# Another order of work for all engines in the transformer stacks: the four groups of small products stand apart

## The chip, the cores and the metric

The kernel runs on one core of a Trainium2 chip. The metric is the device time of one launch in microseconds (us), the median of several runs. TensorE does the matrix products (PE in the profile; PEld is its weight load), VectorE is DVE, ScalarE is ACT, GpSimd is POOL, and SyncE (SP) issues the DMAs. Each engine runs its own instructions in the order in which they are written, and waits on semaphores for the others.

## The reference, cut to what matters

The input x is 4 sequences of 512 tokens with 128 features, float32. Four blocks are added to x one after the other: a retention attention, a stack of six layers, a recurrent mixer, and the same stack again. Only the two stacks are touched here. A layer of the stack is

```
q, k, v = split(shift(x) @ Wqkv)          # 16 heads of 64
q, k = rotary(l2norm(q) * qs), rotary(l2norm(k) * ks)
# windows of 32 queries against the 64 keys of the window before and their own
attn = softmax(mask(8 * q @ k.T)); x = (attn @ v) @ Wo + x
a, gate = split(layernorm(shift(x)) @ W1 + b1)
x = a * gelu(gate) @ W2 + b2 + x
```

## The kernel before, in words

`ffn_stack` (line 347) computes a stack. It is built twice, for the two stacks. Its unit of work is a tile of 128 tokens: 96 tiles per stack (6 layers, 4 sequences, 4 tiles each), 192 in all. Four tiles make a group, for which the feed-forward part is done at 512 columns.

On TensorE a tile needs: six projections `project` (line 577; chunks k0, q0, k1, q1, v0, v1; each 128x128 times 128x512), four times `turn` (585; four 128x128 transposes each), the scores `scores` in two parts (600; 64 small products of 64x64 by 64x32 in all, 8 window-and-row places for 8 head pairs; the trace counts two matmuls and two weight loads for each), two times `turn_probs` (611; four transposes), the values `weigh` in two parts (626; 32 small products each, two matmuls and two loads for each), and `project_out` (640; eight 128x128 products, again two matmuls each). A group adds `center` (647), `variance` (654), six `up` (661) and `down` (670, three products): 11 products of 128x512.

Around them: VectorE does `rotate` (1018, 1020), `sum_squares` (1029), `norms` (1041 to 1052), `mask_max` (1063; it frees the score banks `bank_s`), `sum_probs` (1073), `invert` (1081), `mid` (1091), `mid_norm`, `hidden` and `finish`. ScalarE does `square` (855), `guess`, `keep` (881), `values_out` (889), `exponent` (898), `probs_out` (905), `heads_out` (913) and the group's activations. GpSimd does `stage` (1192), `rope` (1200), `unit` (1210), `off_max` (1218) and `scale_probs` (1226). SyncE spreads the values to their windows by DMA (`spread_values`) once both `values_out` of a tile and `weigh` part 1 of the tile two before it are done, and prefetches the weights of the next layer.

The order is written out by hand, per engine, in a function `slot(N, T, G, at, of)`: one slot per tile, T is N modulo 4. `at(lag)` names the tile that is `lag` slots behind, `of(lag)` the group. So the engines work at several tiles at once: on TensorE before, a slot does the first projections of tile N and the output projection of tile N-6. `slots` (469) writes out 16 slots, then a loop of two rounds of 32 slots, then 28 slots.

The results of projections and transposes go to four PSUM banks `work[0..3]`. TensorE uses them in turn, and ahead of each use waits until the reader of the bank's last content is done; `BANK` tells the readers which bank to take. The scores go to `bank_s[0..1]`, which both parts write and both `mask_max` read; the values go to `bank_o`, which each part of `weigh` fills and `heads_out` empties.

Before, TensorE's slot holds `weigh` part 0 by itself near its start, and `weigh` part 1, `scores` part 0 and `scores` part 1 directly one behind the other near its end.

Of the kernel before, what the change touches and what calls it, by code (L numbers as in the profile page):

```python
# [346 lines left out]
def ffn_stack(nc, shared, w):  # L347

    xo, ident, rot, mask = shared["x"], shared["ident"], shared["rot"], shared["mask"]
    with ExitStack() as ctx:  # L350
# [3 lines left out]
        def ps(name):  # L354
# [58 lines left out]
            "wa1": 3,  # L413
            "t_q0": (1, 3, 2, 1),
            "t_k1": (2, 1, 3, 2),
            "t_q1": (3, 2, 0, 3),
            "p_q0": (0, 3, 0, 3),
            "p_k0": (1, 0, 1, 0),
            "p_v1": (1, 3, 2, 3),
            "wo": (0, 3, 1, 0),  # L420
            "p_v0": (3, 1, 0, 1),
            "wg2": 0,
            "p_q1": (2, 1, 1, 0),
            "pt0": (0, 3, 3, 2),
            "p_k1": (0, 3, 3, 2),
            "t_k0": (2, 0, 3, 2),
            "pt1": (3, 0, 2, 1),
            "wa2": 2,
            "wa0": 3,
            "ct": 2,  # L430
            "va": 3,
            "w2": 3,
            "wg1": 0,
            "wg0": 2,
        }
        FIRST_IN, LAST_IN, LAST_UNIT, FIRST_PV, LAST_PV = "q0", "v0", "q1", 0, 1
# [131 lines left out]
        def _(pe):  # L568
# [104 lines left out]
            def slot(N, T, G, at, of):  # L673
                row = of(0).row
                if T == 0:
                    wait(pe, "pt_set0", N - 5)
                    up(of(3), "lin", 1, work[(0 + row) % 4])
                    wait(pe, "ot_set1", N - 6)
                    weigh(*at(5), 0)
                    wait(pe, "squared_k1", N - 1)  # L680
                    turn(*at(2), "q0", work[(1 + row) % 4])
                    wait(pe, "kept_k0", N - 2)
                    turn(*at(2), "k1", work[(2 + row) % 4])
                    wait(pe, "pt_set1", N - 5)
                    turn(*at(2), "q1", work[(3 + row) % 4])
                    wait_group(pe, "hid1", G - 3)
                    project(*at(0), "q0", work[(0 + row) % 4])
                    wait(pe, "kept_q0", N - 2)
                    project(*at(0), "k0", work[(1 + row) % 4])
                    wait(pe, "kept_k1", N - 2)  # L690
                    project(*at(3), "v1", work[(2 + row) % 4])
                    wait(pe, "kept_q1", N - 2)
                    project_out(*at(6), work[(3 + row) % 4])
                    wait(pe, "squared_q0", N - 0)
                    project(*at(3), "v0", work[(0 + row) % 4])
                    wait(pe, "squared_k0", N - 0)
                    up(of(3), "gate", 2, work[(1 + row) % 4])
                    wait(pe, "v_out1", N - 3)
                    project(*at(0), "q1", work[(2 + row) % 4])
                    wait(pe, "mid_set", N - 6)  # L700
                    turn_probs(*at(4), 0, work[(3 + row) % 4])
                    wait(pe, "v_out0", N - 3)
                    project(*at(0), "k1", work[(0 + row) % 4])
                    wait(pe, "ot_set0", N - 5)
                    weigh(*at(5), 1)
                    wait(pe, "masked1", N - 3)
                    scores(*at(2), 0)
                    scores(*at(2), 1)
                    wait_group(pe, "gelu2", G - 3)
                    turn(*at(1), "k0", work[(1 + row) % 4])  # L710
                    wait(pe, "squared_q1", N - 0)
                    turn_probs(*at(4), 1, work[(2 + row) % 4])
                elif T == 1:
                    wait(pe, "pt_set0", N - 5)
                    up(of(3), "lin", 2, work[(3 + row) % 4])
                    wait(pe, "ot_set1", N - 6)
                    weigh(*at(5), 0)
                    wait(pe, "squared_k1", N - 1)
                    turn(*at(2), "q0", work[(0 + row) % 4])
                    wait(pe, "kept_k0", N - 2)  # L720
                    turn(*at(2), "k1", work[(1 + row) % 4])
                    wait(pe, "pt_set1", N - 5)
                    turn(*at(2), "q1", work[(2 + row) % 4])
                    wait_group(pe, "hid2", G - 3)
                    project(*at(0), "q0", work[(3 + row) % 4])
                    wait(pe, "kept_q0", N - 2)
                    project(*at(0), "k0", work[(0 + row) % 4])
                    wait(pe, "kept_k1", N - 2)
                    project(*at(3), "v1", work[(1 + row) % 4])
                    wait(pe, "kept_q1", N - 2)  # L730
                    project_out(*at(6), work[(2 + row) % 4])
                    wait(pe, "squared_q0", N - 0)
                    project(*at(3), "v0", work[(3 + row) % 4])
                    wait(pe, "squared_k0", N - 0)
                    up(of(3), "lin", 0, work[(0 + row) % 4])
                    wait(pe, "v_out1", N - 3)
                    project(*at(0), "q1", work[(1 + row) % 4])
                    wait(pe, "mid_set", N - 6)
                    turn_probs(*at(4), 0, work[(2 + row) % 4])
                    wait(pe, "v_out0", N - 3)  # L740
                    project(*at(0), "k1", work[(3 + row) % 4])
                    wait_group(pe, "hid0", G - 3)
                    center(of(2), work[(0 + row) % 4])
                    wait(pe, "ot_set0", N - 5)
                    weigh(*at(5), 1)
                    wait(pe, "masked1", N - 3)
                    scores(*at(2), 0)
                    scores(*at(2), 1)
                    wait(pe, "squared_q1", N - 0)
                    variance(of(2), work[(1 + row) % 4])  # L750
                    wait(pe, "pt_set0", N - 4)
                    turn(*at(1), "k0", work[(2 + row) % 4])
                    wait(pe, "squared_k1", N - 0)
                    turn_probs(*at(4), 1, work[(3 + row) % 4])
                elif T == 2:
                    wait_group(pe, "center_set", G - 2)
                    down(of(3), work[(0 + row) % 4])
                    wait(pe, "ot_set1", N - 6)
                    weigh(*at(5), 0)
                    wait_group(pe, "std_read", G - 2)  # L760
                    turn(*at(2), "q0", work[(1 + row) % 4])
                    wait(pe, "kept_k0", N - 2)
                    turn(*at(2), "k1", work[(2 + row) % 4])
                    wait(pe, "pt_set1", N - 5)
                    turn(*at(2), "q1", work[(3 + row) % 4])
                    wait_x(pe, G - 3)
                    project(*at(0), "q0", work[(0 + row) % 4])
                    wait(pe, "kept_q0", N - 2)
                    project(*at(0), "k0", work[(1 + row) % 4])
                    wait(pe, "kept_k1", N - 2)  # L770
                    project(*at(3), "v1", work[(2 + row) % 4])
                    wait(pe, "kept_q1", N - 2)
                    project_out(*at(6), work[(3 + row) % 4])
                    wait(pe, "squared_q0", N - 0)
                    project(*at(3), "v0", work[(0 + row) % 4])
                    wait(pe, "squared_k0", N - 0)
                    project(*at(0), "q1", work[(1 + row) % 4])
                    wait(pe, "v_out1", N - 3)
                    turn_probs(*at(4), 0, work[(2 + row) % 4])
                    wait(pe, "mid_set", N - 6)  # L780
                    project(*at(0), "k1", work[(3 + row) % 4])
                    wait(pe, "ot_set0", N - 5)
                    weigh(*at(5), 1)
                    wait(pe, "masked1", N - 3)
                    scores(*at(2), 0)
                    scores(*at(2), 1)
                    wait(pe, "v_out0", N - 3)
                    turn(*at(1), "k0", work[(0 + row) % 4])
                    wait(pe, "squared_q1", N - 0)
                    turn_probs(*at(4), 1, work[(1 + row) % 4])  # L790
                elif T == 3:
                    wait(pe, "pt_set0", N - 5)
                    up(of(2), "gate", 1, work[(2 + row) % 4])
                    wait(pe, "ot_set1", N - 6)
                    weigh(*at(5), 0)
                    wait(pe, "squared_k1", N - 1)
                    turn(*at(2), "q0", work[(3 + row) % 4])
                    wait(pe, "kept_k0", N - 2)
                    up(of(2), "gate", 0, work[(0 + row) % 4])
# [47 lines left out]
        def _(act):  # L847
# [110 lines left out]
            def slot(N, T, G, at, of):  # L958
                keep(*at(2), "k0")
                probs_out(*at(5), 1)  # L960
                if T == 3:
                    gelu(of(2), 1)
# [1379 lines left out]
```

## Time and profile before

| | us |
|---|---|
| median of 3 runs | 3958.96 (3957.44 to 3965.38) |
| the profiled execution's own time | 3964.79 |
| its span in the trace | 3963.0 |
| PE busy | 3592.3 (91%) |
| DVE busy | 3253.2 (82%) |
| POOL busy | 2634.9 (66%) |
| ACT busy | 2372.4 (60%) |

The busy shares are averages over both stacks, the mixer between them (about 1800 to 2260 us) and the retention block ahead of them. In the page's 40 slices PE stands at nine tenths or more in nearly all slices of the stacks, DVE at eight, POOL at seven or eight.

### The profile page before, as it was taken

Reading aid. Unit: us, or ns where it says so; the run is one execution under the profiler, and the core shown is the slowest. Engines: PE = TensorE matmul, PEld = TensorE weight load, DVE = VectorE, ACT = ScalarE, POOL = GpSimd, SP = SyncE. Lnnn points to the kernel's source line nnn. Section 1 sums busy time; section 2 is a strip of 40 time slices with the busy share of each in tenths; the row PEclk is TensorE's granted clock in tenths of the full one; section 3 lists DMA queues with packets and bytes.
Section 4 is the critical chain, followed back from the end, with each engine's and each line's share of the span. In section 5 each row is a group of like instructions: output and inputs, shape, how many; then the busy total and the mean of one; then the engine's idle time right before and its main releaser. Section 6 shows DMA issues by size and latency. Waiting matters only on the chain. (4 is left out here: it accounts for less than half of the span.)

```text
span 3963.0 us, 156885 instructions
## 1 busy us (share of the span) xinstructions
PE 3592.3 (91%) x61680; PEld 2388.6 (60%) x61680; DVE 3253.2 (82%) x11525; ACT 2372.4 (60%) x4337; POOL 2634.9 (66%) x2556
## 2 busy tenths in 40 slices
PE   6799999999999999987699589999999999999997
PEld 4466666666666666652465356666666666666664
DVE  6888888888888888854899688888887888888884
ACT  2466667666666666663422156666666667666664
POOL 1787878877788778743000188787877788877872
PEclk9899999999999999997799689999999999999999
DMA  1232322322322322220000023233232232322222
GB/s 52 59 82 68 81 73 73 80 71 68 79 73 72 78 72 67 67 56 15 1 1 6 28 64 80 62 84 77 71 80 67 73 82 73 78 71 70 66 65 55
DMA packets 170283, 250.91 MB, mean 63 GB/s; under 512 B 36544, under 2 KB 67264, under 8 KB 169408
## 3 DMA queue, kind: packets, MB, share of 16 engines
q1 hardware_dynamic: 169536, 240.72, 24.4%
q8 instruction: 497, 8.14, 0.9%
q14 instruction: 250, 2.05, 0.2%
HBM read 38.21 MB, written 1.05 MB: 10 GB/s over the span
## 5 line engine op out<-in xcount | busy, mean ns | idle before, releaser
L1200 POOL TENSOR_TENSOR stack_roped<-stack_rot_c,stack_rot_s 128x512 f32<-128x512 f32 x768 | 966.3, 1273 | 420.9 <-DVE stack_rot_s L1020 420.9
L577 PE MATMUL stack_work<-stack_w_qkv,stack_xs 128*128 128x512 f32 x2304 | 1122.1, 603 | 36.3 <-ACT stack_sq L855 21.0
L1210 POOL TENSOR_TENSOR stack_roped<-stack_roped,stack_rnorm 128x512 f32<-128x512 f32 x768 | 784.6, 1043 | 175.9 <-DVE stack_rnorm L1052 175.9
L1018 DVE TENSOR_TENSOR stack_rot_c<-stack_work,rot_tables 128x512 f32<-128x512 f32 x768 | 518.3, 675 | 259.7 <-PE stack_work L577 256.5
L855 ACT ACTIVATE stack_sq<-stack_work 128x512 f32<-128x512 f32 x768 | 451.2, 598 | 367.7 <-DVE stack_rot_s L1020 367.6
L577 PEld LDWEIGHTS stack_work<-stack_w_qkv,stack_xs 128*128 128x128 f32 x2304 | 396.6, 193 | 335.1 <-issue 323.7
L626 PEld LDWEIGHTS stack_bank_o<-stack_p_t,stack_v_w 64*64 64x64 f32 x24576 | 405.4, 136 | 314.9 <-issue 308.8
L1063 DVE CUSTOM_DVE_ANT_0 stack_s_m<-stack_bank_s,band 128x64 f32<-128x64 f32 x3072 | 469.6, 218 | 137.4 <-PE stack_bank_s L600 126.0
L1029 DVE TENSOR_REDUCE stack_ssq<-stack_sq 128x8 f32<-128x512 f32 x768 | 519.8, 677 | 6.9 <-issue 6.6
L1020 DVE TENSOR_TENSOR stack_rot_s<-stack_work,rot_tables 128x512 f32<-128x512 f32 x768 | 522.0, 680 | 0.0
L1218 POOL TENSOR_TENSOR stack_s_m<-stack_s_m,stack_smax 128x512 f32<-128x512 f32 x384 | 421.2, 1097 | 114.9 <-DVE stack_smax L1063 113.5
L626 PE MATMUL stack_bank_o<-stack_p_t,stack_v_w 64*64 64x32 f32 x24576 | 452.1, 222 | 15.3 <-issue 14.3
L585 PE MATMUL stack_work<-ident,stack_roped 128*128 128x128 f32 x3072 | 436.0, 283 | 18.9 <-issue 13.9
L881 ACT COPY stack_q_t<-stack_work 128x512 f32<-128x512 f32 x384 | 228.4, 595 | 351.1 <-PE stack_work L585 350.8
L640 PEld LDWEIGHTS stack_work<-stack_o_t,stack_w_o 128*128 128x128 f32 x3072 | 372.7, 192 | 96.0 <-issue 94.9
L600 PE MATMUL stack_bank_s<-stack_k_t,stack_q_t 64*32 64x64 f32 x24576 | 322.2, 225 | 112.0 <-issue 111.5
L1226 POOL TENSOR_TENSOR stack_s_m<-stack_s_m,stack_inv 128x512 f32<-128x512 f32 x384 | 400.8, 1044 | 9.4 <-DVE stack_inv L1081 9.4
L585 PEld LDWEIGHTS stack_work<-ident,stack_roped 128*128 128x128 f32 x3072 | 343.7, 143 | 94.5 <-issue 66.4
L640 PE MATMUL stack_work<-stack_o_t,stack_w_o 128*128 128x128 f32 x3072 | 374.4, 275 | 3.6 <-issue 1.9
L600 PEld LDWEIGHTS stack_bank_s<-stack_k_t,stack_q_t 64*32 64x32 f32 x24576 | 275.5, 105 | 142.5 <-issue 133.3
L661 PE MATMUL stack_work<-stack_x_c,stack_w 128*128 128x512 f32 (+1 forms) x576 | 312.2, 625 | 23.6 <-issue 15.4
L881 ACT COPY stack_k_t<-stack_work 128x512 f32<-128x512 f32 x384 | 224.6, 585 | 147.4 <-PE stack_work L585 141.9
(247 smaller groups left out, 5193.0 us busy)
## 6 DMA issues: line engine op xcount, KB each, us to landing
stack_v_w<-stack_v_nat SPq DMA_DIRECT2D x1152, 128.0 KB
stack_v_w<-stack_v_nat SPq DMA_DIRECT2D x768, 64.0 KB
stack_w_qkv<-table_ffn_qkv SPq DMA_DIRECT2D x192, 96.0 KB, 2.1
stack_w_o<-table_ffn_wo SPq DMA_DIRECT2D x12, 512.0 KB, 4.4
stack_w<-table_ffn_w SPq DMA_DIRECT2D x12, 384.0 KB, 3.2
stack_w<-table_ffn_w SPq DMA_DIRECT2D x12, 192.0 KB, 2.9
x_outer<-L_attn_a_X SPq DMA_DIRECT2D x4, 256.0 KB, 7.5
ret_xpos<-table_xpos SPq DMA_DIRECT2D x1, 1024.0 KB, 6.8
```

What stands on the lines that cost most here:

```text
L577: pe.matmul(bank[:, :], xs[:, T, :], w_qkv[:, g.half, col:col + 512], start=True, stop=True).then_inc(done["proj_" + c], 1)
L585: last = pe.transpose(bank[:, P * n:P * (n + 1)], roped[:, CHUNKS.index(c), T % 2, P * n:P * (n + 1)], ident[:, :])
L600: last = pe.matmul(bank_s[j][WINDOW * n:WINDOW * (n + 1), 64 * hp:64 * hp + 64], q_t[rows, T % 2, hp, WINDOW * n:WINDOW * (n + 1)], k_t[ro ...
L626: last = pe.matmul(bank_o[HD * odd:HD * (odd + 1), gp, at:at + WINDOW], v_w[64 * gp:64 * gp + 64, T % 2, n, 2 * m + j, :], p_t[64 * gp:64 ...
L640: last = pe.matmul(bank[:, 0:P], w_o[:, g.half, n, :], o_t[:, T % 2, n, :], start=n == 0, stop=n == PAIRS - 1)
L881: act.copy(out, src).then_inc(done["kept_" + c], 1)
L1018: dve.tensor_tensor(rot_c[:, i % 2, :].rearrange("p (h d) -> p h d", h=8), src.rearrange("p (h d) -> p h d", h=8), cosine, ALU.mult)
L1020: dve.tensor_tensor(rot_s[:, i % 2, :].rearrange("p (h f d) -> p h f d", h=8, f=2), src.rearrange("p (h f d) -> p h f d", h=8, f=2)[:, :, ...
L1029: dve.tensor_reduce(ssq[:, T % 2, i, :], sq[:, i % 2, :].rearrange("p (h d) -> p h d", h=8), AX.X, ALU.add).then_inc(done["summed_" + c], 1)
L1063: last = dve.tensor_tensor_reduce(s_m[:, T % 2, j, hp, :], bank_s[j][:, 64 * hp:64 * hp + 64], mask[:, first:first + 2 * WINDOW], 1.0, LOW ...
L1200: pool.tensor_tensor(roped[:, i, T % 2, :], rot_c[:, i % 2, :], rot_s[:, i % 2, :], ALU.add).then_inc(done["roped_" + c], 1)
L1210: pool.tensor_tensor(r, r, rnorm[:, T % 2, i, :].unsqueeze(2).broadcast_to([P, 8, HD]), ALU.mult).then_inc(done["united_" + c], 1)
```

## The change

Only the order and the lags change; no operation is added or dropped. On TensorE a slot now reads, without its waits (T = 1; the feed-forward products of the other T stand at like places):

```
project q1 (tile N-3), up, project v1 (N-5),
weigh part 1 (N-7),
turn q0, turn k0 (N-4), turn_probs 1 (N-6), turn q1 (N-4), project k0, project q0 (N-2),
scores part 0 (N-4),
turn_probs 0 (N-6), project_out (N-7),
weigh part 0 (N-6),
turn k1 (N-4), project k1 (N-2), project v0 (N-4),
scores part 1 (N-4), up
```

The core of the diff:

```diff
-        FIRST_IN, LAST_IN, LAST_UNIT, FIRST_PV, LAST_PV = "q0", "v0", "q1", 0, 1
+        FIRST_IN, LAST_IN, LAST_UNIT, FIRST_PV, LAST_PV = "k0", "v1", "k1", 0, 1
...
-                    wait(pe, "ot_set0", N - 5)
-                    weigh(*at(5), 1)
-                    wait(pe, "masked1", N - 3)
-                    scores(*at(2), 0)
-                    scores(*at(2), 1)
...
+                    wait(pe, "ot_set0", N - 7)
+                    weigh(*at(7), 1)
...
+                    wait(pe, "masked1", N - 5)
+                    scores(*at(4), 0)
+                    wait(pe, "pt_set1", N - 6)
+                    turn_probs(*at(6), 0, work[(0 + row) % 4])
+                    wait(pe, "kept_q1", N - 4)
+                    project_out(*at(7), work[(1 + row) % 4])
+                    wait(pe, "ot_set1", N - 7)
+                    weigh(*at(6), 0)
...
+                    project(*at(4), "v0", work[(0 + row) % 4])
+                    scores(*at(4), 1)
```

The table `BANK`, the four `slot` functions of TensorE (T = 0 to 3) and those of ScalarE, VectorE and GpSimd are rewritten to match. The one of VectorE, new:

```
mid_norm, finish (T == 2); sum_squares k1, q1 (N-2); norms 0 (N-2); hidden 1 (T == 1);
rotate k0, q0 (N-1); norms 1; mid (N-6); norms 2; sum_squares k0 (N-1); norms 3;
sum_probs 1 (N-4); rotate k1 (N-1); sum_probs 0; invert 1; sum_squares q0 (N-1);
hidden 2 (T == 0) or hidden 0 (T == 3); rotate q1 (N-1); invert 0; mask_max 0, 1 (N-3)
```

The one of ScalarE: center_out and inv_std (T == 3), gelu 1 (T == 1), square q1, values_out 1, keep q0 and k0, heads_out 1, gain_bias (T == 3), probs_out 1, keep q1, table load (T < 2), guess, probs_out 0, exponent 0, square k0 and q0, exponent 1, heads_out 0, keep k1, center_square (T == 2), square k1, gelu 2 (T == 0), values_out 0, gelu 0 (T == 3). The one of GpSimd: stage, rope k0 and q0, unit q0 and k0, scale_probs 1, unit q1, scale_probs 0, rope k1 and q1, off_max 0, unit k1, off_max 1. A slot of VectorE or GpSimd runs beside TensorE's slot of the next number. The down product of a group moves from T == 2 to T == 3.

## Rows read from the trace of the kernel before

**Rows 1.** Busy time of each engine in a steady stretch (x instructions), clock, DMA.
```profile
300.00:1500.00 1200.00, 1140.41 (x21952) 773.70 (x21951) 1016.86 (x3888) 800.72 (x1474) 938.73 (x910) 0.99 0.30 74
```

**Rows 2.** TensorE's groups in the same stretch: count | busy, mean ns | idle before.
```profile
L626 PE MATMUL stack_bank_o<-stack_p_t,stack_v_w 64*64 64x32 f32 x8960 | 164.3, 221 | 4.5 <-issue 4.2
L585 PE MATMUL stack_work<-ident,stack_roped 128*128 128x128 f32 x1120 | 159.3, 283 | 7.1 <-issue 7.1
L640 PE MATMUL stack_work<-stack_o_t,stack_w_o 128*128 128x128 f32 x1120 | 136.3, 275 | 0.0
L600 PE MATMUL stack_bank_s<-stack_k_t,stack_q_t 64*32 64x64 f32 x8960 | 118.3, 225 | 41.1 <-issue 40.8
L661 PE MATMUL stack_work<-stack_x_c,stack_w 128*128 128x512 f32 (+1 forms) x210 | 111.7, 613 | 6.9 <-issue 6.9
```

**Rows 3.** TensorE's waits in the whole kernel: total us, times, longest.
```profile
PE stack_bank_s L600 <- issue: 111.5, 81, 2.2
...
PE stack_bank_o L626 <- issue: 14.3, 30, 1.3
```

**Rows 4.** Timeline of TensorE through most of a slot: start us, us, instruction, count.
```profile
1005.10 1.53 PE L585 MATMUL stack_work<-ident,stack_roped 128*128 128x128 f32 x12
1006.47 2.74 PE L577 MATMUL stack_work<-stack_w_qkv,stack_xs 128*128 128x512 f32 x6
1009.05 1.95 PE L640 MATMUL stack_work<-stack_o_t,stack_w_o 128*128 128x128 f32 x16
1010.83 1.88 PE L577 MATMUL stack_work<-stack_w_qkv,stack_xs 128*128 128x512 f32 x4
1012.55 0.60 PE L611 MATMUL stack_work<-ident,stack_s_m 128*128 128x128 f32 x4
1012.99 1.02 PE L577 MATMUL stack_work<-stack_w_qkv,stack_xs 128*128 128x512 f32 x2
1013.94 1.13 PE L626 MATMUL stack_bank_o<-stack_p_t,stack_v_w 64*64 64x32 f32 x64
1015.01 1.57 PE L600 MATMUL stack_bank_s<-stack_k_t,stack_q_t 64*32 64x64 f32 x128
1016.50 0.66 PE L585 MATMUL stack_work<-ident,stack_roped 128*128 128x128 f32 x4
1017.00 0.60 PE L611 MATMUL stack_work<-ident,stack_s_m 128*128 128x128 f32 x4
```

**Rows 5.** The same one slot later, with a stop inside the scores.
```profile
1029.57 1.14 PE L626 MATMUL stack_bank_o<-stack_p_t,stack_v_w 64*64 64x32 f32 x64
1030.63 1.26 PE L600 MATMUL stack_bank_s<-stack_k_t,stack_q_t 64*32 64x64 f32 x101
1033.63 0.55 PE L600 MATMUL stack_bank_s<-stack_k_t,stack_q_t 64*32 64x64 f32 x27 [1.74 <-issue]
```

**Rows 6.** Timeline: a wide product directly behind the scores.
```profile
1068.31 1.13 PE L654 MATMUL stack_work<-stack_c_sq,stack_mean_m 128*128 128x512 f32 x2
1069.28 0.60 PE L585 MATMUL stack_work<-ident,stack_roped 128*128 128x128 f32 x4
```

**Rows 7.** DMA queues, whole kernel: packets, MB, share of the engines.
```profile
q8 instruction: 497, 8.14, 0.9%
```

**Rows 8.** DMA view, 1029.00 to 1033.63 us, 40 slices; then its instruction packets.
```profile
GB/s 0 0 0 0 0 0 0 0 0 0 0 0 0 0 0 142 0 0 0 0 0 0 0 0 0 0 177 248 124 18 0 0 0 0 0 88 195 212 71 0
...
q8 instruction: 1, 0.02, 1.8%
```

**Rows 9.** Timeline of VectorE: eight maskings start, the next work; a rotation.
```profile
1001.71 0.22 DVE L1063 CUSTOM_DVE_ANT_0 stack_s_m<-stack_bank_s,band 128x64 f32<-128x64 f32 x1
...
1002.87 0.90 DVE L1100 TENSOR_TENSOR stack_x_c<-stack_x_c,stack_std 128x512 f32<-128x512 f32 x1
...
1007.53 0.69 DVE L1018 TENSOR_TENSOR stack_rot_c<-stack_work,rot_tables 128x512 f32<-128x512 f32 x1 [1.06 <-PE stack_work L577]
...
1008.74 0.19 DVE L1081 RECIPROCAL stack_inv<-stack_psum_p 128x8 f32<-128x8 f32 x1
```

**Rows 10.** TensorE in the first stack: first projections, and the first output projection.
```profile
107.35 1.98 PE L577 MATMUL stack_work<-stack_w_qkv,stack_xs 128*128 128x512 f32 x4 [1.80 <-ACT stack_xst L1001]
...
187.35 1.95 PE L640 MATMUL stack_work<-stack_o_t,stack_w_o 128*128 128x128 f32 x16
```

More of the change, by code:

```diff
@@ L412, in ffn_stack @@
         BANK = {
[L413 to L434, printed above, removed]
+            "p_q1": (1, 1, 0, 3),
+            "p_v1": (2, 0, 0, 3),
+            "t_q0": (3, 3, 1, 1),
+            "t_k0": (0, 0, 2, 2),
+            "pt1": (3, 3, 2, 2),
+            "t_q1": (2, 2, 1, 1),
+            "p_k0": (1, 1, 3, 3),
+            "p_q0": (2, 2, 0, 0),
+            "pt0": (0, 0, 2, 2),
+            "wo": (1, 3, 3, 2),
+            "t_k1": (3, 3, 2, 2),
+            "p_k1": (2, 2, 0, 0),
+            "wg2": 3,
+            "p_v0": (2, 1, 1, 1),
+            "wa0": 1,
+            "wg1": 3,
+            "wa2": 0,
+            "wa1": 2,
+            "ct": 1,
+            "va": 0,
+            "w2": 2,
+            "wg0": 1,
         }
-        FIRST_IN, LAST_IN, LAST_UNIT, FIRST_PV, LAST_PV = "q0", "v0", "q1", 0, 1
+        FIRST_IN, LAST_IN, LAST_UNIT, FIRST_PV, LAST_PV = "k0", "v1", "k1", 0, 1
         def wait(eng, name, tile):
@@ L675, in slot @@
                 if T == 0:
[L676 to L685, printed above, removed]
@@ L686, in slot @@
-                    wait_group(pe, "hid1", G - 3)
[L687 to L703, printed above, removed]
@@ L704, in slot @@
-                    wait(pe, "ot_set0", N - 5)
-                    weigh(*at(5), 1)
-                    wait(pe, "masked1", N - 3)
-                    scores(*at(2), 0)
-                    scores(*at(2), 1)
[L709 to L755, printed above, removed]
-                    wait_group(pe, "center_set", G - 2)
-                    down(of(3), work[(0 + row) % 4])
-                    wait(pe, "ot_set1", N - 6)
-                    weigh(*at(5), 0)
-                    wait_group(pe, "std_read", G - 2)
[L761 to L765, printed above, removed]
-                    wait_x(pe, G - 3)
[L767 to L799, printed above, removed]
-                    wait(pe, "pt_set1", N - 5)
-                    turn(*at(2), "k1", work[(1 + row) % 4])
-                    wait_group(pe, "gelu1", G - 2)
-                    turn(*at(2), "q1", work[(2 + row) % 4])
-                    wait(pe, "kept_q0", N - 2)
-                    project(*at(0), "q0", work[(3 + row) % 4])
-                    wait_group(pe, "gelu0", G - 2)
-                    project(*at(0), "k0", work[(0 + row) % 4])
-                    wait(pe, "kept_k1", N - 2)
-                    project(*at(3), "v1", work[(1 + row) % 4])
-                    wait(pe, "kept_q1", N - 2)
-                    project_out(*at(6), work[(2 + row) % 4])
-                    wait(pe, "squared_q0", N - 0)
-                    project(*at(3), "v0", work[(3 + row) % 4])
-                    wait(pe, "squared_k0", N - 0)
-                    project(*at(0), "q1", work[(0 + row) % 4])
-                    wait(pe, "v_out1", N - 3)
-                    turn_probs(*at(4), 0, work[(1 + row) % 4])
-                    wait(pe, "mid_set", N - 6)
-                    project(*at(0), "k1", work[(2 + row) % 4])
-                    wait(pe, "ot_set0", N - 5)
-                    weigh(*at(5), 1)
-                    wait(pe, "masked1", N - 3)
-                    scores(*at(2), 0)
-                    scores(*at(2), 1)
-                    wait(pe, "v_out0", N - 3)
-                    turn(*at(1), "k0", work[(3 + row) % 4])
-                    wait(pe, "squared_q1", N - 0)
-                    turn_probs(*at(4), 1, work[(0 + row) % 4])
@@ new lines, in slot @@
+                    wait(pe, "kept_k1", N - 5)
+                    project(*at(3), "q1", work[(0 + row) % 4])
+                    wait(pe, "squared_k1", N - 3)
+                    project(*at(5), "v1", work[(1 + row) % 4])
+                    wait(pe, "ot_set0", N - 7)
+                    weigh(*at(7), 1)
+                    wait_group(pe, "gelu0", G - 3)
+                    turn(*at(4), "q0", work[(2 + row) % 4])
+                    wait(pe, "v_out0", N - 5)
+                    turn(*at(4), "k0", work[(3 + row) % 4])
@@ new lines, in slot @@
+                    wait(pe, "squared_q1", N - 3)
+                    turn_probs(*at(6), 1, work[(0 + row) % 4])
+                    wait(pe, "v_out1", N - 5)
+                    turn(*at(4), "q1", work[(1 + row) % 4])
+                    wait(pe, "kept_q0", N - 4)
+                    project(*at(2), "k0", work[(2 + row) % 4])
+                    wait(pe, "kept_k0", N - 4)
+                    project(*at(2), "q0", work[(3 + row) % 4])
+                    wait(pe, "masked1", N - 5)
+                    scores(*at(4), 0)
@@ new lines, in slot @@
+                    wait(pe, "pt_set1", N - 6)
[4 more added lines that the diff above has]
+                    weigh(*at(6), 0)
+                    wait(pe, "squared_k0", N - 2)
+                    turn(*at(4), "k1", work[(2 + row) % 4])
+                    wait(pe, "squared_q0", N - 2)
+                    project(*at(2), "k1", work[(3 + row) % 4])
@@ new lines, in slot @@
+                heads_out(*at(7), 1)
+                if T == 3:
+                    gain_bias(of(2))
+                probs_out(*at(6), 1)
+                keep(*at(4), "q1")
+                if T == 0 and live_group(G - 2):
+                    act.preload_act_table_set(TABLE)
+                if T == 1 and live_group(G - 3):
+                    act.preload_act_table_set(TABLE)
+                guess(*at(3))
+                probs_out(*at(6), 0)
+                exponent(*at(5), 0)
+                square(*at(2), "k0")
@@ L964, in slot @@
+                square(*at(2), "q0")
+                exponent(*at(5), 1)
+                heads_out(*at(6), 0)
+                keep(*at(4), "k1")
+                if T == 2:
+                    center_square(of(2))
+                square(*at(2), "k1")
+                if T == 0:
+                    gelu(of(3), 2)
+                values_out(*at(4), 0)
                 if T == 3:
                     gelu(of(2), 0)
-                keep(*at(2), "k1")
-                keep(*at(2), "q1")
-                if T == 1 and live_group(G - 3):
-                    act.preload_act_table_set(TABLE)
@@ L1122, in slot @@
             def slot(N, T, G, at, of):
-                if T == 1:
-                    hidden(of(3), 2)
-                sum_squares(*at(1), "k1")
-                if T == 0:
-                    hidden(of(3), 1)
-                mask_max(*at(3), 1)
                 if T == 2:
```

212 lines of the change are left out of this document (158 added, 54 removed).

## The prediction

> **What bounds the kernel now.** I read the page first: PE is busy for 91% of the span. Then I asked for a stretch inside the first stack. Between 300 and 1500 us PE is busy for 1140.4 of 1200 us, DVE for 1016.9, POOL for 938.7, ACT for 800.7, at a granted clock of 0.99, that is the upper of its two levels, 2.4 GHz [rows 1]. Line 640 has 16 matmuls a tile, so its 1120 are 70 tiles [rows 2], and a tile takes 1200 / 70 = 17.14 us. DVE needs 14.5 us of that, POOL 13.4, ACT 11.4. PE sets the pace, so I ask what PE's 17.14 us consist of.
>
> PE's idle time in this stretch is 59.6 us, and all of it is "issue", with no engine waited for: 41.1 before score products, 4.5 before value products, 7.1 and 6.9 before lines 585 and 661 [rows 2]. In the whole kernel it is 81 stops of up to 2.2 us in the scores and 30 in the values [rows 3]. The timeline shows what PE does without a stop, as distances from one start to the next [rows 4]: a projection (2.58 / 3) 0.86 us, four transposes 0.44, the output projection 1.78, a part of `weigh` 1.07, both parts of `scores` 1.49. A tile is then 6 x 0.86 + 6 x 0.44 + 1.78 + 2 x 1.07 + 1.49 + 11 x 0.86 / 4 = 15.57 us. The small products also cost at their borders. The projection ahead of `weigh` takes 0.95 instead of 0.86, so entering costs 0.09. Twelve transposes behind `weigh` take 1.37 instead of 1.32 and four behind `scores` 0.50 instead of 0.44, so leaving costs 0.06 [rows 4]; leaving to a wide product costs 0.11 (0.97 instead of 0.86) [rows 6]. Two entries and two exits a tile make 0.3, and the sum is 15.86. So 17.14 - 15.86 = 1.28 us of each tile is lost in stops and slow stretches. Of this I put 14.0 / 70 = 0.20 (lines 585 and 661, stops not inside small products, in part the loop's jump) aside as staying. 1.08 us a tile belongs to the small products.
>
> **What the stops are.** A stop is in the middle of a run of like products: 101 of 128 score matmuls run, then 1.74 us of nothing, then 27 more [rows 5]. The instruction queue moved 8.14 MB in 497 packets [rows 7], 16.4 KB each. PE's 61,680 matmuls and as many weight loads make 248 a packet, its waits come on top, so I read a packet as about 256 of PE's instructions. In the window with the stop one such packet moves; it is the single slice at 1030.8 us (the 16th of 0.116 us, 142 GB/s) [rows 8], and PE goes on at 1033.63, 2.8 us after it. At the stop PE has gone through 64 + 101 matmuls and as many loads since 1029.57, 330 instructions; 256 back from it is 1030.2, in `weigh`. So from the start of a block of instructions until the next is usable take about 3.4 us, and a block must last that long. `weigh` part 1 and both `scores` are 384 instructions within 1.07 + 1.49 = 2.56 us. Stops there are bound to come, in the slots where a block ends in them.
>
> The Trainium skill (Runtime: NRT & Kernel Launch, "Instruction fetch mechanics") says that instructions arrive in blocks of 256 and that crossing to the next is mostly hidden, since engines take them more slowly than they are fetched. By that the stops would be of another origin and stay; the rows agree on the block's size, but not on its being hidden. This is the last rival below.
>
> **The change part by part.** Groups of small products, 128 instructions each, now stand apart. How fast can 256 instructions pass? Behind `scores` 0 come `turn_probs` and `project_out` (40 instructions and two waits, 0.44 + 1.78), then `weigh` 0: 128 + 42 + 86 instructions in 0.78 + 2.28 + 0.72 = 3.8 us. Behind `scores` 1 come q1 and v1 (1.8 us, 10 instructions) and `weigh` 1: 0.78 + 1.9 + 1.0 = 3.7 us, with an up product between them 4.5. Behind `weigh` 0: turn k1, project k1 and v0, 2.2 us: 1.07 + 2.2 + 0.6 = 3.9. Behind `weigh` 1 four turns and two projections, 3.5 us: above 5. The shortest are all above 3.4, but not by much, and only blocks that begin in a narrow part of the order meet them, about 130 of some 640 instructions of a tile. If such a block misses by 0.2 us on average, that is 130 / 256 x 0.2 = 0.1 us a tile. Bounds: 0, and 0.4 if they miss by 0.8.
>
> - Gain: 1.08 us for 86 tiles of each stack (the first and last ten run differently): -186 us. Remaining waits +0.12 x 172 = +21 us (0 to +69).
> - Borders: before there are two separate clusters a tile, now four. Two more entries cost 2 x 0.09 = 0.18. Of exits there were `weigh` 0 (0.06) and `scores` (mostly 0.06, with T = 1 0.11), now three to transposes at 0.06 and one, behind `scores` 1, to a wide product at 0.11: +0.16. The scores are cut in two: 101 matmuls start within 1.26 - 0.22 = 1.04 us and 27 within 0.33 [rows 5], so 128 need 1.37 and the group takes 1.49; 0.12 is the emptying at its end, and it comes a second time. In all +0.46 us a tile, x 192 = +88 us. No row shows an entry into `scores` from a wide product or into `weigh` from line 640; bounds 0.30 (they are free in part) and 0.65 (each twice as dear): +58 to +125.
>
> The Trainium skill (TensorEngine Tiling (Array Packing), "Key Properties") says that a change of tiling mode drains the TensorE. A tile has five such changes before (one is between `weigh` and `scores`) and eight after. The rows show about 0.15 us for one of them; without this rule the sum would be 88 us lower, so it is the rule that speaks against this change.
>
> - Start and end of a stack: before, 80.0 us pass from the first projections to the first `project_out` [rows 10], six slots. Now the first projection is in slot 2 and the first `project_out` in slot 7, five slots. A filling slot is about 80 / 6 = 13 us, but much of it is work that then comes later; I take -7 us a stack, -15 in all (bounds -40 and +15, if the deeper lags lengthen the end).
> - Other engines: their work is the same. A rotation costs 1.2 us and starts 0.2 behind the projection's end (start at 1006.47, 0.86 long, start of the rotation at 1007.53); `mask_max` costs 1.16 a part [rows 9]. The tightest loop that I find is through the score banks. From the end of `scores` 1, q1 is projected (0.97), VectorE rotates it (0.2 + 1.2), inverts (0.1) and masks twice (2.3): 4.8 us, 5.0 with a semaphore. TensorE reaches `scores` 0, which waits for that, after q1, v1, `weigh` 1, four turns, k0 and q0: 0.97 + 0.95 + 1.07 + 1.82 + 1.8 = 6.6 us. 1.6 us are to spare. The other DVE work of a slot, 14.5 - 3.6 = 10.9, fits into the 16.4 - 3.7 = 12.7 us between; with T = 2, where `mid_norm` is followed by a wait for `down`, I find some 0.5 us to spare. So I cost it at nothing; if this cover is gone, PE waits for `masked1` with all its queue behind it.
> - SP: `spread_values` waits for v1, now projected in slot N+5; `weigh` 0 of that tile is a slot and more later, over 16 us for ten DMAs. Nothing.
>
> Sum: 3963.0 - 186 + 21 + 88 - 15 = 3871 us of span. The profiled execution's own time is 1.8 above its span, and 5.8 above the median of the runs: 3871 + 1.8 - 5.8 = 3867, rounded **3865 us**, 2.4% faster. A tile then takes 17.14 - 1.08 + 0.12 + 0.46 = 16.6 us.
>
> **The rivals.**
> - *More of it*: entries at the low bound (-30), no remaining waits (-21), a shorter fill (-15): 3800. For it: the shortest blocks are above 3.4 us. Against: each is a bound.
> - *Half apart*: blocks of 3.7 to 3.9 us are still too short. For it: 30 stops stand in value products [rows 3], most of them in the `weigh` part 0 that stands by itself, so the distance to the cluster before it did not always suffice. Remaining 0.4 us a tile: +48, 3915.
> - *Another engine's chain*: DVE at 14.5 of 16.6 us is 87% busy in a fixed order. If its waits for q1, `down` and `project_out` add 0.5 us a tile that PE must wait for, 0.5 x 192 = 96 is given back: 3960, no change. Against: I find slack in each loop.
> - *Slower*: the stops belong to the small products, not to their crowding, and move with them; then nothing is won and the borders are paid: 3959 + 88 - 15 = 4030. It decides if 1 us a tile still stands before lines 600 and 626. Against: the values, with as many instructions as the scores, had 30 short stops against 81 long ones.
>
> **How the numbers follow.** Forecast 0.55, more of it 0.17, half apart 0.10, another chain 0.10, slower 0.08. A measurement of this kernel tells about 0.2% (8 us) from no change. Faster: 0.55 + 0.17 + 0.10 + a third of the chain case = 0.85; same 0.05; slower 0.10. The range 3795 to 3945 leaves out the slower case, most of the chain case, and a little below. The forecast's own range is 3830 to 3900.
>
> **What would show it.** Right: the 81 stops before line 600 fall to under 20, issue before 600 and 626 together from 126 to under 30 us; entries of 0.09 before all four groups; the two `scores` parts at about 0.8 us each; 1200 us hold 72 to 73 tiles; DVE busy in steady stretches 87%; no line of PE waiting on `smax`. Wrong: stops unchanged; a PE wait for DVE over 0.3 us a tile; parts of `scores` at 1 us; a fill longer than 80 us.

## The result, and the profile after

The changed kernel takes 3854.12 us (median of 4 runs, 3845.62 to 3856.61); before, beside it, 3962.17. The ratio is 0.9734, with an interval of 0.9705 to 0.9764: 2.7% faster, where 2.4% and 3865 us were forecast. A second set of runs, on the chip of later experiments, gave 0.9758 (0.9736 to 0.9779). The profiled execution's span is 3843.8 us, 119 below the one before; the medians are 108 us apart, since the profiled execution after was the fastest of its four. The medians in this document leave out slow runs; there was one, of the first experiment (5059 us at a granted clock of 0.65).

The same steady stretch as in [rows 1], busy time of PE, PEld, DVE, ACT and POOL with their instructions, then clock, DMA share and GB/s:

```profile
300.00:1500.00 1200.00, 1188.86 (x22787) 785.34 (x22788) 1062.45 (x4033) 830.00 (x1524) 973.68 (x944) 1.00 0.31 76
```

PE's groups in it, as [rows 2]:

```profile
L626 PE MATMUL stack_bank_o<-stack_p_t,stack_v_w 64*64 64x32 f32 x9344 | 166.5, 221 | 0.0
L640 PE MATMUL stack_work<-stack_o_t,stack_w_o 128*128 128x128 f32 x1152 | 140.4, 275 | 0.0
L600 PE MATMUL stack_bank_s<-stack_k_t,stack_q_t 64*32 64x64 f32 x9280 | 124.7, 224 | 0.0
L661 PE MATMUL stack_work<-stack_x_c,stack_w 128*128 128x512 f32 (+1 forms) x218 | 116.2, 615 | 7.4 <-ACT stack_hid L955 7.4
```

PE is busy for 1188.9 us instead of 1140.4. The idle time before the scores, 41.1 us, is 0.0; before the values it was 4.5 and is 0.0. The one new item is 7.4 us before the up products, for which ScalarE's gelu is to blame. DVE is busy for 89% of the stretch instead of 85%. In the whole kernel, as [rows 3]:

```profile
L626 PE MATMUL stack_bank_o<-stack_p_t,stack_v_w 64*64 64x32 f32 x24576 | 437.4, 221 | 1.4 <-issue 1.4
L661 PE MATMUL stack_work<-stack_x_c,stack_w 128*128 128x512 f32 (+1 forms) x576 | 309.5, 621 | 27.8 <-ACT stack_hid L955 21.3 <-DVE stack_xst L1118 3.2 <-DVE stack_hid L1109 1.7
L600 PE MATMUL stack_bank_s<-stack_k_t,stack_q_t 64*32 64x64 f32 x24576 | 330.9, 224 | 0.0
```

The 81 stops in the scores (111.5 us) are gone, and of the 14.3 us in the values 1.4 are left.

A second thing went with the stops: time at the lower clock. Before, directly behind the stop of [rows 5], the timeline of PE and, as in [rows 1], a stretch with its clock (the third figure from the end; 0.50 is 1.2 GHz) read:

```profile
1034.11 1.11 PE L585 MATMUL stack_work<-ident,stack_roped 128*128 128x128 f32 x4
1035.01 1.06 PE L611 MATMUL stack_work<-ident,stack_s_m 128*128 128x128 f32 x4
1034.00:1037.00 3.00, 3.00 (x21) 2.10 (x10) 1.84 (x17) 1.17 (x2) 2.98 (x4) 0.50 0.55 137
```

Four transposes take 0.90 us there, where the same place one slot earlier shows 0.50 [rows 4]. The clock fell behind this stop of 1.74 us, and not behind the one of 1.33 us two slots later. Added up over windows of 5 us, from 300 to 1650 and from 2400 to 3700 us, PE was at 1.2 GHz for 68 us before and for 10 us after. At half speed that is worth at most 29 us of the gain, an estimate from these two numbers.

The timeline of PE through a slot shows what the borders cost, again as distances from one start to the next:

```profile
1001.60 1.88 PE L577 MATMUL stack_work<-stack_w_qkv,stack_xs 128*128 128x512 f32 x4
1003.41 1.13 PE L626 MATMUL stack_bank_o<-stack_p_t,stack_v_w 64*64 64x32 f32 x64
1004.47 1.09 PE L585 MATMUL stack_work<-ident,stack_roped 128*128 128x128 f32 x8
1005.40 0.60 PE L611 MATMUL stack_work<-ident,stack_s_m 128*128 128x128 f32 x4
...
1007.14 1.88 PE L577 MATMUL stack_work<-stack_w_qkv,stack_xs 128*128 128x512 f32 x4
1008.95 0.86 PE L600 MATMUL stack_bank_s<-stack_k_t,stack_q_t 64*32 64x64 f32 x64
1009.74 0.66 PE L611 MATMUL stack_work<-ident,stack_s_m 128*128 128x128 f32 x4
1010.23 1.95 PE L640 MATMUL stack_work<-stack_o_t,stack_w_o 128*128 128x128 f32 x16
1012.11 1.14 PE L626 MATMUL stack_bank_o<-stack_p_t,stack_v_w 64*64 64x32 f32 x64
1013.18 0.66 PE L585 MATMUL stack_work<-ident,stack_roped 128*128 128x128 f32 x4
1013.67 1.02 PE L577 MATMUL stack_work<-stack_w_qkv,stack_xs 128*128 128x512 f32 x2
...
1015.39 1.02 PE L577 MATMUL stack_work<-stack_w_qkv,stack_xs 128*128 128x512 f32 x2
1016.34 0.86 PE L600 MATMUL stack_bank_s<-stack_k_t,stack_q_t 64*32 64x64 f32 x64
1017.13 1.13 PE L577 MATMUL stack_work<-stack_w_qkv,stack_xs 128*128 128x512 f32 x2
1018.09 1.02 PE L654 MATMUL stack_work<-stack_c_sq,stack_mean_m 128*128 128x512 f32 x2
```

Two projections ahead of a small group take 1.81 us, not 1.72: an entry of 0.09, into the scores as into the values. From line 640 into `weigh` it is 1.88 for 1.78, so 0.10. A part of the scores takes 0.79, two of them 1.58 where both together took 1.49. The four transposes behind a group take 0.49 for 0.44, the projection behind scores 1 takes 0.96 for 0.86.

The start of a stack, as [rows 10]:

```profile
107.71 0.70 PE L577 MATMUL stack_work<-stack_w_qkv,stack_xs 128*128 128x512 f32 x1 [1.73 <-ACT stack_xst L1001]
...
171.09 1.17 PE L640 MATMUL stack_work<-stack_o_t,stack_w_o 128*128 128x128 f32 x9
```

63.4 us instead of 80.0.

Where the 119 us came from, from the starts of lines 834, 640 and 842 in both timelines (both stacks together): until the first output projection -37; from there to the seventh from the end, 89 tiles a stack, -99; from that one to the last, where PE now works through deeper lags, +21; behind them -6. Unrounded that makes -120.4, and about 1 us was lost outside the stacks. In the 89 tiles a tile takes 16.45 us instead of 17.02.

### The profile page after: what moved, and what is told of

Read it like the earlier page. It is cut to its first block and busy times, and to the rows that moved or that the text cites. A ratio compares the mean times of both kernels' runs of the same rounds, so it can differ in the third digit from the quotient of the medians.

```text
span 3843.8 us, 156883 instructions
## 1 busy us (share of the span) xinstructions
PE 3600.5 (94%) x61680; PEld 2342.3 (61%) x61680; DVE 3283.2 (85%) x11525; ACT 2374.7 (62%) x4335; POOL 2637.5 (69%) x2556
## 5 line engine op out<-in xcount | busy, mean ns | idle before, releaser
L577 PE MATMUL stack_work<-stack_w_qkv,stack_xs 128*128 128x512 f32 x2304 | 1142.0, 602 | 35.3 <-ACT stack_sq L855 19.0
L1200 POOL TENSOR_TENSOR stack_roped<-stack_rot_c,stack_rot_s 128x512 f32<-128x512 f32 x768 | 983.6, 1303 | 145.2 <-DVE stack_rot_s L1020 144.9
L1029 DVE TENSOR_REDUCE stack_ssq<-stack_sq 128x8 f32<-128x512 f32 x768 | 496.5, 667 | 6.3 <-issue 4.7
L626 PEld LDWEIGHTS stack_bank_o<-stack_p_t,stack_v_w 64*64 64x64 f32 x24576 | 394.9, 135 | 171.7 <-issue 147.3
L585 PE MATMUL stack_work<-ident,stack_roped 128*128 128x128 f32 x3072 | 453.6, 281 | 8.5 <-issue 5.9
L1063 DVE CUSTOM_DVE_ANT_0 stack_s_m<-stack_bank_s,band 128x64 f32<-128x64 f32 x3072 | 449.4, 216 | 7.4 <-PE stack_bank_s L600 7.4
L626 PE MATMUL stack_bank_o<-stack_p_t,stack_v_w 64*64 64x32 f32 x24576 | 437.4, 221 | 1.4 <-issue 1.4
L1218 POOL TENSOR_TENSOR stack_s_m<-stack_s_m,stack_smax 128x512 f32<-128x512 f32 x384 | 400.6, 1043 | 2.9 <-DVE stack_smax L1063 2.7
L640 PEld LDWEIGHTS stack_work<-stack_o_t,stack_w_o 128*128 128x128 f32 x3072 | 358.1, 192 | 3.3 <-DVE stack_hid L1109 3.3
L661 PE MATMUL stack_work<-stack_x_c,stack_w 128*128 128x512 f32 (+1 forms) x576 | 309.5, 621 | 27.8 <-ACT stack_hid L955 21.3
L600 PE MATMUL stack_bank_s<-stack_k_t,stack_q_t 64*32 64x64 f32 x24576 | 330.9, 224 | 0.0
L905 ACT COPY stack_p_t<-stack_work 128x512 f32<-128x512 f32 x384 | 228.9, 596 | 56.6 <-PE stack_work L611 56.3
```

Of the source, the lines that this page charges most:

```text
L577: pe.matmul(bank[:, :], xs[:, T, :], w_qkv[:, g.half, col:col + 512], start=True, stop=True).then_inc(done["proj_" + c], 1)
L585: last = pe.transpose(bank[:, P * n:P * (n + 1)], roped[:, CHUNKS.index(c), T % 2, P * n:P * (n + 1)], ident[:, :])
L600: last = pe.matmul(bank_s[j][WINDOW * n:WINDOW * (n + 1), 64 * hp:64 * hp + 64], q_t[rows, T % 2, hp, WINDOW * n:WINDOW * (n + 1)], k_t[ro ...
L626: last = pe.matmul(bank_o[HD * odd:HD * (odd + 1), gp, at:at + WINDOW], v_w[64 * gp:64 * gp + 64, T % 2, n, 2 * m + j, :], p_t[64 * gp:64 ...
L640: last = pe.matmul(bank[:, 0:P], w_o[:, g.half, n, :], o_t[:, T % 2, n, :], start=n == 0, stop=n == PAIRS - 1)
L1029: dve.tensor_reduce(ssq[:, T % 2, i, :], sq[:, i % 2, :].rearrange("p (h d) -> p h d", h=8), AX.X, ALU.add).then_inc(done["summed_" + c], 1)
```

## The experiments

Three theories stood against each other. **Blocks**: PE stops when some 256 of its instructions pass in less than the 3.4 us in which the next ones come. **Rival A**: PE stops where two groups of small products touch. **Rival B**: the other engines' new order and the deeper lags bring the gain. The first four kernels ran on one chip, where the kernel before had a median of 3941.62 us.

**The change with the scores joined again**, here T = 0.

```diff
-                    wait(pe, "masked1", N - 5)
-                    scores(*at(4), 0)
...
                     project(*at(4), "v0", work[(1 + row) % 4])
+                    wait(pe, "masked1", N - 5)
+                    scores(*at(4), 0)
                     scores(*at(4), 1)
```

> The changed kernel with the two parts of the scores put together again (part 0 moved down to stand directly ahead of part 1); 256 instructions in one run, the values stay apart. Theory (TensorE stops where a block of some 256 instructions passes faster than the next arrives, about 3.4 us): only a block that begins within some 20 instructions around the start of the run fits in it, so about 0.08 stops of 1.3 us a tile, +0.1 us; one entry (0.09), one exit (0.06) and one emptying (0.12) fewer, -0.27 us a tile. About 15 stops in the scores, 3825 us (3805 to 3840). Rival A (stops come wherever two groups touch): half of the stops of before, 40, and 3890. Rival B (what helped is the new order of the other engines and the deeper lags, not the distance): no stop comes back, 3802.

Measured: 3876.25 us, ratio 0.9834 (0.9814 to 0.9854), slower than the change. The time missed the theory, though hardly a stop came back in the scores (in the values there are 5.2 us of them, in the changed kernel 1.4):

```profile
L600 PE MATMUL stack_bank_s<-stack_k_t,stack_q_t 64*32 64x64 f32 x24576 | 291.6, 225 | 1.7 <-issue 1.6
L661 PE MATMUL stack_work<-stack_x_c,stack_w 128*128 128x512 f32 (+1 forms) x576 | 308.3, 619 | 35.8 <-ACT stack_hid L955 29.2 <-DVE stack_xst L1118 3.2 <-DVE stack_hid L1109 2.5
L611 PE MATMUL stack_work<-ident,stack_s_m 128*128 128x128 f32 x1536 | 233.9, 275 | 26.6 <-DVE stack_hid L1109 20.5 <-DVE stack_xst L1118 2.7 <-issue 1.4
```

Busy time of the scores fell by 39 us, but PE waits 20.5 us for VectorE ahead of `turn_probs` 0, and more than before for ScalarE (29.2 for 21.3 ahead of the up products, 30.1 for 19.0 ahead of projections). By the code, scores 0 no longer fills 0.8 us ahead of the turn whose bank VectorE has to clear, so PE comes to it too soon. Rival A expected 40 stops where two parts of 128 instructions touch, and there are 1.6 us of them: it falls for this pair. The place of scores 0 in the changed kernel thus seems to have a use that I had not named: cover for VectorE.

**The change with the old trio restored**: additionally, `weigh(*at(6), 1)` directly behind scores 1.

> The changed kernel with the trio of before restored in it: scores 0, scores 1 and weigh 1 directly one behind the other (384 instructions in 2.56 us), weigh 0 by itself; everything else as changed. Theory (blocks): the stops of before come back, 0.8 to 1.1 us a tile, the borders of before too (-0.46 us a tile): 3854 - 88 + 170 = 3935 us (3910 to 3970), 70 or more stops over 0.15 us in lines 600 and 626. Rival B (the other engines' order and the lags bring the gain): few stops, 3854 - 88 = 3766.

Measured: 4137.56 us, ratio 1.0500 (1.0476 to 1.0523). The waits of PE:

```profile
PE stack_bank_o L626 <- issue: 106.0, 89, 2.9
PE stack_work L611 <- DVE stack_hid L1109: 49.1, 46, 2.9
PE stack_work L585 <- ACT stack_sq L855: 37.4, 53, 2.7
```

89 stops of 106.0 us are back, now in the values, which stand last in the run of 384. Against the kernel above, that has 5.2 us of issue there, this is +101 us. Rival B, which expected few stops with all other orders as changed, falls. The total was missed by 200 us. The other part is waits for VectorE and ScalarE, by the code since q1 is now projected behind `weigh` and what hangs on it comes later, and the clock: in the windows named above PE was at 1.2 GHz for 112 us, for 10 in the changed kernel. So this run gives the number of stops but not their price.

**The kernel before with one group moved.** `weigh` part 1 and its wait move up in each T, nothing else; here T = 0:

```diff
+                    wait(pe, "ot_set0", N - 5)
+                    weigh(*at(5), 1)
                     wait(pe, "v_out1", N - 3)
                     project(*at(0), "q1", work[(2 + row) % 4])
                     wait(pe, "mid_set", N - 6)
                     turn_probs(*at(4), 0, work[(3 + row) % 4])
                     wait(pe, "v_out0", N - 3)
                     project(*at(0), "k1", work[(0 + row) % 4])
-                    wait(pe, "ot_set0", N - 5)
-                    weigh(*at(5), 1)
                     wait(pe, "masked1", N - 3)
```

> The kernel before with one edit: weigh part 1 stands ahead of project q1, so that q1, turn_probs 0 and k1 lie between it and the scores; all other orders, lags and banks as before. Theory (blocks): the run shrinks from 384 to 256 instructions, stops in line 600 fall from 81 to under 20, those in line 626 stay at about 30; -0.75 us a tile of stops, +0.2 us a tile for one entry and one exit more: 3962 - 129 + 38 = 3870 us (3845 to 3895). Rival B (the gain needs the other engines' new order and lags): as before, 3962, or slower. Rival A (stops wherever two groups touch): 40 stops, 3930.

Measured: 3824.52 us, ratio 0.9702 (0.9683 to 0.9720). That is 20 us below the expected band, but the kernel before, too, was 20 us faster on this chip: as a ratio it lies at the band's lower edge (3845 / 3962 = 0.9705).

```profile
L626 PE MATMUL stack_bank_o<-stack_p_t,stack_v_w 64*64 64x32 f32 x24576 | 447.1, 221 | 13.9 <-issue 12.9
L600 PE MATMUL stack_bank_s<-stack_k_t,stack_q_t 64*32 64x64 f32 x24576 | 323.3, 225 | 2.3 <-issue 2.2
```

With one group moved and all else as before, the 111.5 us of stops in the scores are 2.2, and the whole gain is there. This is the plainest evidence: neither the other engines' orders, nor the lags, nor the splitting of the scores is needed for it. The time at 1.2 GHz went with the stops here too, from 68 to 14 us.

**The change with two pairs**: weigh 0 with scores 0, scores 1 with weigh 1.

> The changed kernel with two pairs in place of four single groups: weigh 0 and scores 0 together, scores 1 and weigh 1 together, 256 instructions each. Theory (blocks): two entries and two exits fewer, -0.35 us a tile, 67 us; blocks that fit in a pair are rare, +0.15 to 0.3 us a tile: 3815 us (3790 to 3840), 20 to 40 stops. Rival A (touching groups stop): 80 stops, 3920. Rival B: no stops, 3787.

Measured: 4042.10 us, ratio 1.0260 (1.0239 to 1.0282).

```profile
PE stack_work L611 <- DVE stack_hid L1109: 49.5, 46, 2.9
PE stack_work L585 <- ACT stack_sq L855: 38.4, 57, 1.8
PE stack_bank_s L600 <- issue: 34.4, 28, 2.4
PE stack_work L611 <- ACT stack_sq L855: 25.7, 91, 0.5
...
PE stack_bank_o L626 <- issue: 18.4, 40, 1.7
```

68 stops of 52.8 us, between the theory's 20 to 40 and rival A's 80; 27 of them last over 0.9 us, and many of the others under 0.2. With them come 113.6 us of waits for other engines that no theory had. A miss in time for all three; it shows mainly how little this order tolerates a move.

The next four ran on another chip, before at 3950.05 us.

**Both value groups apart**: the kernel with one move, `weigh(*at(5), 0)` also behind the three turns.

> The kernel with weigh part 1 ahead of project q1 (the run e3_before_values_apart), and weigh part 0 also moved: behind the three turns, ahead of project q0, 1.3 us and 24 instructions further from the scores of the slot before. Theory (blocks of 256 instructions need about 3.4 to 4.5 us): the 29 stops of 12.9 us left in line 626 go, and the slowed loads beside them, -0.15 us a tile; its exit is to a projection (0.11) in place of a transpose (0.06), +0.05: 0.1 us a tile, 20 us below the run with one move, ratio to before 0.965. Rival A (stops wherever groups touch): the stops in line 626, which touches nothing, stay; ratio 0.972.

```profile
L626 PE MATMUL stack_bank_o<-stack_p_t,stack_v_w 64*64 64x32 f32 x24576 | 436.0, 220 | 2.2 <-issue 2.1
L585 PE MATMUL stack_work<-ident,stack_roped 128*128 128x128 f32 x3072 | 429.1, 278 | 41.9 <-ACT stack_hid L955 31.0 <-ACT stack_sq L855 6.5 <-ACT stack_k_t L881 3.8
```

Measured: 3855.67 us, ratio 0.9773 (0.9746 to 0.9799). The stops went as expected, 12.9 us became 2.1; the time did not follow, it is above the run with one move (0.9702) instead of below. The turns come 1.1 us sooner, and PE waits there 31.0 us for gelu.

**One projection between**: the kernel before, `weigh` 1 ahead of project k1 only, so that 4 instructions and 0.95 us stand between it and the scores (with T = 1 `center` as well).

> The kernel before with one smaller edit: weigh part 1 is moved ahead of project k1 only, so that one projection (4 instructions, 0.95 us) lies between it and the scores. Theory (blocks): a block across it now takes about 2.5 us instead of 1.6, still under 3.4: stops stay frequent, 60 to 80 of them, but 0.9 us shorter each, from 1.4 to 0.5 to 0.8 us: 81 x 1.4 = 111 us become 35 to 55; +0.1 us a tile for the entry into the scores: 3941 - 65 + 19 = 3895 us, ratio 0.988 (0.980 to 0.993). Rival A (stops where groups touch): nothing touches weigh any more, so all stops go as in the run with two more groups between, ratio 0.970. Rival B: no change, 1.000.

```profile
PE stack_bank_s L600 <- issue: 26.4, 50, 1.7
```

Measured: 3864.50 us, ratio 0.9787 (0.9761 to 0.9813). 81 stops of 1.38 us on average became 50 of 0.53. Rival A, for which nothing touched any more, expected none, and falls. The theory has the direction, and the size only roughly. Read one by one, 70 of the 81 stops last over 1 us, 1.55 on average; taking 0.95 us from each stop would leave 67 of at least 0.15 us, 42 us in all (an estimate from that list), where 50 with 26.4 us were measured. That the two averages differ by about one projection is in part chance, since they are over different sets of stops. The ratio is just below the expected band.

**The change, gelu 2 earlier.**

```diff
-                square(*at(2), "k1")
                 if T == 0:
                     gelu(of(3), 2)
+                square(*at(2), "k1")
```

> The changed kernel, with ScalarE's gelu 2 (T == 0) moved ahead of square k1. Theory: TensorE's wait for it (46 times 0.46 us before up gate 1 in T == 1, seen as 21.3 us, with a start 0.6 us late) goes, since gelu 2 with its table load ends about 0.6 us sooner; square k1 ends later, and project q1 waits for it with little to spare: -15 to -25 us, ratio to before 0.968. Rival: the wait changes over to square k1 and nothing is won, 0.973.

```profile
L661 PE MATMUL stack_work<-stack_x_c,stack_w 128*128 128x512 f32 (+1 forms) x576 | 309.3, 621 | 9.7 <-DVE stack_xst L1118 3.2 <-ACT stack_hid L955 3.2 <-DVE stack_hid L1109 1.7
```

Measured: 3819.71 us, ratio 0.9669 (0.9644 to 0.9693). PE's wait for gelu fell from 21.3 to 3.2 us. The medians are 33 us (0.9%) apart, the spans of the two profiled executions 17.8 us, which is what the wait explains. The profiled execution was the slowest of the four of this kernel (3831.07 us; the others 3816 to 3822), so what the rest of the 33 us is stays open.

**The change once more.**

> The changed kernel once more, on the same chip as the others, to compare with them: ratio to before 0.9734 as on record (0.9705 to 0.9764).

Measured: 3852.99 us, ratio 0.9758 (0.9736 to 0.9779).

So the change with gelu earlier (0.9669) is faster than the change beside it (0.9758). The kernel before with one move (0.9702) is at least as good as the change: its interval, 0.9683 to 0.9720, meets the lower end of 0.9705 to 0.9764 and lies below 0.9736 to 0.9779, but it never ran on the same chip as the change. Whether it or the change with gelu earlier is better is open as well, since those two intervals overlap.

**Where the stops stand, in the trace of the kernel before.** If only the length of the run mattered, every tile would stop, and at the same place. Instead, over long stretches, every second tile stops, and each time a little earlier in the run, as the number of matmuls left behind the stop shows (x27, then 30, 36, 39):

```profile
1033.63 0.55 PE L600 MATMUL stack_bank_s<-stack_k_t,stack_q_t 64*32 64x64 f32 x27 [1.74 <-issue]
1067.93 0.45 PE L600 MATMUL stack_bank_s<-stack_k_t,stack_q_t 64*32 64x64 f32 x30 [1.33 <-issue]
1101.93 0.74 PE L600 MATMUL stack_bank_s<-stack_k_t,stack_q_t 64*32 64x64 f32 x36 [1.79 <-issue]
1136.78 0.65 PE L600 MATMUL stack_bank_s<-stack_k_t,stack_q_t 64*32 64x64 f32 x39 [1.42 <-issue]
```

Between one and the next lie 1245 or 1246 matmuls and weight loads. With some 34 waits, which the profile does not count, that would be five blocks of 256 (an estimate). The same 27, 30, 36, 39 stand at 485.98 to 586.55 us and, in the second stack, at 2645.77 to 2745.45. One packet of the instruction queue moves about 2.6 us ahead of 1067.93 and 2.3 us ahead of 1101.93, as one did 2.8 us ahead of 1033.63. So where PE stops hangs on the place in its stream of instructions, which neither rival gives a reason for.

## Why the prediction was right, point by point

- *PE sets the pace, and 1.08 us of a tile is stops at the small products.* Right. The move of one group alone brings the 111.5 us of idle time before the scores down to 2.2 and makes the kernel 3.0% faster.
- *A stop is a block of 256 instructions that passes too fast.* Held in the counts of stops, except for the two pairs, where 68 came instead of 20 to 40: 384 in a run stop 81 and 89 times, 256 in a run (scores alone) hardly, and one projection put into the run shortens the stops. The places of the stops in the kernel before step through the program as blocks would. That the packet seen ahead of a stop is the block PE lacks is inferred from its size and time, not shown directly, and the 3.4 us come from a single stop.
- *Remaining waits 0.12 us a tile* (its own product gives 0.1). Too careful: 1.4 us are left in the whole kernel. By the theory, the shortest blocks, 3.7 us, suffice.
- *Borders +0.46 us a tile.* Measured from the rows above: entries 0.09 and 0.10 for the two more (0.19), the scores' second emptying 0.09 for 0.12, exits about as forecast (0.16; 0.05 and 0.10 each for 0.06 and 0.11). That is some 0.44. The remark on the drain reads 0.15 us for one change of mode; by its rows that is an entry and an exit together.
- *Start and end, -15 us.* Together they gave -22, but by two halves that were each mis-sized: the start alone gives -37 (16.6 us in the first stack instead of 7). A filling slot costs 13 us, five instead of six save one, and little of it came later. The end gave 15 us back: the last six steps from one output projection to the next are 21 us longer, 6 us are won behind them.
- *Other engines at nothing.* Right for the score banks: no wait for masking. But I listed DVE's loops and did not follow ScalarE's gelu through T = 0 into the up product of T = 1: 46 waits, 21.3 us, and 17.8 us between the spans of the runs with and without most of them (33 between the medians).
- *Sum.* In the middle a tile was to save 1.08 - 0.12 - 0.46 = 0.50 us and saved 0.56 (17.02 to 16.45). Add the borders (0.44) and the missed wait (21.3 / 178 = 0.12), and what the stops were worth comes to 1.12 us, for 1.08. That the sum is so near is in part luck: the remaining waits of 0.12 that did not come cancel the wait for gelu of 0.12 that did.
- *What the 1.08 us consist of.* I called it stops and slow stretches and did not follow the second of the two. Idle time before lines 600 and 626 is 0.65 us a tile of it (125.8 us became 1.4, over 192 tiles), and the lower clock is at most 0.16 (29 us over 178). I read a mean granted clock of 0.99 as the upper level and missed that it holds stretches at 1.2 GHz. The rest, some 0.3 us, stays open; part of it is scores groups that took up to 1.79 us without a listed stop, where an undisturbed one takes 1.57.

The rival *half apart* fell, *another engine's chain* was right in kind and small in size. *Slower* fell: the stops did not move along with the small products, they went. What the runs add to the reason is that the change is much larger than its gain needs.

The Trainium skill (Runtime: NRT & Kernel Launch, "Instruction fetch mechanics") has crossings from one block of 256 instructions to the next as mostly hidden. The places of the stops agree with such a block; with three groups in one run the crossing was not hidden, if the reading above is right (111.5 us in 81 stops), and with the groups apart it was (0.0 us before the scores).

## What to carry to other kernels

On an engine that is full, look for idle time ahead of its own instructions that nothing released, and count instructions, not only time: here a run of 384 instructions, short products and their loads, passing in 2.56 us, stopped 81 times in 192 tiles, most likely because it outran the supply of instructions. One group taken out of it mended it; one projection put into it left 50 shorter stops. See whether such stops step through the program from one round to the next, and look at the granted clock behind them in short windows, since a mean of 0.99 hides it. Cut such a run once, since each further separate group costs its entry and exit, and a cut its emptying, here up to 0.3 us. Where the order is written by hand and banks are shared in turn, try the one move alone first; moving a group also moves what the other engines hang on its neighbours.

## What the runs showed that I had not expected

- Joined scores do not have one price. In the kernel with one move they take 323.3 us of busy time for 192 tiles, 1.68 each; in the change with the scores joined 291.6 us, 1.52 each. Both are the same 128 matmuls a tile with almost no stop over 0.15 us, and both kernels show a granted clock of 1.00 between 300 and 1500 us. Cut in two they take 330.9 us, 0.86 a part. So what makes them slower in the order of the kernel before is not their being joined, and it stays open.
- A scores group in a run of 256 behind few instructions had 1.6 and 2.2 us of stops in all, so a block of nearly the whole run is rarer than my count of about 15 such blocks.
- Moving two small groups of 0.8 to 1.1 us within the changed order (the two pairs) brought 113.6 us of waits for other engines in three places, 49.5 us of it in a single one (46 waits for `hidden`, up to 2.9 us each).
